# A fused graph-attention and mixture-of-experts kernel: VectorE's step without a cast, an addition and three signals; weights loaded by expert; two blocks' rows sent among the last dispatches

## The reference

```python
# layer 1, graph attention on the layer-normalised x
Wh = h @ W;  e = leaky_relu(Wh @ a[:D] + (Wh @ a[D:]).T, 0.2)
alpha = softmax(where(adj > 0, e, -inf));  x = x + elu(alpha @ Wh)
# layer 2, mixture of 8 experts on the layer-normalised x, the best 2 of each token
scores = h @ Wg.T + bg;  top2, idx = top_k(scores, 2);  p = softmax(top2)
x = x + sum over the two experts e of  p_e * (relu(h @ W1[e].T + b1[e]) @ W2[e].T + b2[e])
```

## Time and profile before

| | before |
|---|---|
| median of 3 runs | 440.71 us (440.66 to 441.59) |
| profiled execution | 442.13 us, span 440.3 us |
| busy: TensorE / VectorE / ScalarE / GpSimd | 407.3 / 358.9 / 321.3 / 289.0 us |
| mean granted TensorE clock | 0.991 |
| transfers | 63.04 MB |
| chain that ended last | TensorE 63%, VectorE 20%, ScalarE 5%, DMA 5%, issue 4% |

### The profile page before, as it was taken

One profiled execution on the slowest core, in us unless ns is written; L12 is line 12 of the kernel. 1 busy time (PEld: TensorE's weight loads), 2 busy tenths in 40 slices (PEclk: granted clock), 3 DMA queues, 4 the chain that ended last, 5 costly groups with the idle time before them and its releaser, 6 DMA issues.

```text
span 440.3 us, 9161 instructions
## 1 busy us (share of the span) xinstructions
PE 407.3 (93%) x2272; PEld 308.3 (70%) x2290; DVE 358.9 (82%) x1410; ACT 321.3 (73%) x760; POOL 289.0 (66%) x292
## 2 busy tenths in 40 slices
PE   7998999889998888999999999999999999999980
PEld 3656666666666665688878888888888888876630
DVE  5689999999998898999887887777778778757683
ACT  2678887888888987688888678778767877866500
POOL 1041777777777777777777777767667657764662
PEclk9999999999999999999999999999999999999996
DMA  5995334333333344443632433322233233297888
GB/s 181 293 390 193 102 115 118 108 103 104 100 101 104 97 128 122 128 133 98 200 99 95 122 102 101 115 90 84 91 90 90 66 84 90 79 289 247 248 310 316
DMA packets 44004, 63.04 MB, mean 143 GB/s; under 512 B 7744, under 2 KB 24512, under 8 KB 43712
## 3 DMA queue, kind: packets, MB, share of 16 engines
q1 hardware_dynamic: 30448, 34.88, 26.5%
q0 software_dynamic: 9344, 20.10, 13.6%
q10 hardware_dynamic: 4176, 7.66, 5.3%
HBM read 27.28 MB, written 26.94 MB: 123 GB/s over the span
## 4 chain that ended last, share of the span: by engine, by line
PE 63%; DVE 20%; ACT 5%; DMA 5%; issue 4%; SPq 1%; POOL 1%; DVEq 0%; ACTq 0%; POOLq 0%
PE bank L1441 7%; PE bank L1455 7%; PE bank L1454 7%; PE bank L1457 7%; PE bank L1445 7%; PE bank L1442 7%; PE bank L1425 3%; PE bank L1433 3%; PE bank L1403 3%; PE bank L1316 3%; DVE xn L1066 3%; PE bank L1401 3%; DVE bn L901 2%; DVE neg_max L1048 2%; DVE score L1043 2%
## 5 line engine op out<-in xcount | busy, mean ns | idle before, releaser
L520 POOL DMA_INDIRECT expert_slots<-rows,slot_i x128 | 126.4, 987 | 55.4 <-issue 33.5
L712 ACT ACTIVATE yb<-bank,b_sb 128x512 f32<-128x512 f32 x36 | 24.8, 688 | 51.8 <-PE bank L1457 51.8
L1454 PE MATMUL bank<-hh,w_hi 128*128 128x512 f32 x144 | 60.1, 417 | 0.0
L1441 PE MATMUL bank<-xh,w_hi 128*128 128x512 f32 x144 | 58.5, 406 | 0.9 <-ACT xh L697 0.5
L1455 PE MATMUL bank<-hh,w_lo 128*128 128x512 f32 x144 | 57.4, 398 | 0.0
L1445 PE MATMUL bank<-xl,w_hi 128*128 128x512 f32 x144 | 56.9, 395 | 0.2 <-DVE xl L1122 0.2
L1457 PE MATMUL bank<-hl,w_hi 128*128 128x512 f32 x144 | 56.8, 395 | 0.3 <-DVE hl L1153 0.3
L1442 PE MATMUL bank<-xh,w_lo 128*128 128x512 f32 x144 | 56.8, 395 | 0.0
L536 POOL DMA_INDIRECT moe_rows<-hrelu,ysi x40 | 41.2, 1030 | 17.6 <-issue 10.7
L536 POOL DMA_INDIRECT moe_rows<-hexp,ysi x40 | 40.9, 1023 | 17.7 <-issue 10.1
L1146 DVE CAST hh<-z 128x512 fp32r<-128x512 f32 x36 | 16.5, 459 | 42.3 <-ACT z L702 41.9
(11 more groups left out here) (166 smaller groups left out, 1051.0 us busy)
## 6 DMA issues: line engine op xcount, KB each, us to landing
rows<-xn SPq DMA_DIRECT2D x32, 256.0 KB
xs<-expert_slots SPq DMA_DIRECT2D x27, 260.0 KB
x_all<-x SPq DMA_DIRECT2D x16, 256.0 KB, 3.5
w_raw<-w_t SPq DMA_DIRECT2D x2, 2048.0 KB, 13.7
w_raw<-moe_rows SPq DMA_DIRECT2D x16, 256.0 KB, 4.5
out<-x_all ACTq DMA_DIRECT2D x16, 256.0 KB, 4.7
xs<-expert_slots ACTq DMA_DIRECT2D x11, 260.0 KB
w_hi<-moe_rows SPq DMA_DIRECT2D x9, 256.0 KB, 4.1
```

Of the source, the lines that this page charges most:

```text
L520: nc.gpsimd.indirect_dma_start(out=slots, out_offset=bass.IndirectOffsetOnAxis(ap=slot_i[q][:, k * SUB + j:k * SUB + j + 1], axis=0), in_= ...
L712: nc.scalar.activation(yb[:, :], ps_y[:, :], ACT.Identity, bias=b2_sb[:, e:e + 1]).then_inc(yb_ok, 1)
L1441: nc.tensor.matmul(ps_h[c][:, :], w1_hi[:, e, chunk], xh[:, :], start=True, stop=False)
L1454: nc.tensor.matmul(ps_y[:, :], w2_hi[:, e, c, :], hh[:, c, :], start=c == 0, stop=False)
```

## The change

Four edits. On VectorE, the chosen experts' numbers are compared as the 32-bit integers that the top-8 search delivers, without a copy to float32; the two variances of a step lie in one buffer and get their epsilon in one instruction in place of two; and the three signals to `met` are gone. On SyncE, the weights are loaded expert by expert, two transfers of 256 KB behind each of the first eight groups' row copies, in place of two of 2 MB ahead of them; the loop of copies is written out. On GpSimd, the rows of block 0 are sent after the dispatches of group 14, and the rows of block 1 between the two halves of group 15's dispatches, instead of after all dispatches; sends from block 2 on follow. ScalarE's wait for the weights counts eight transfers.

```diff
+            for g in range(SURE_GROUPS + 1):
+                pass_on(g // 2, g % 2)
+                if g < E:
+                    sp.dma_start(w1_raw[:, g, :], w1_t[:, g, :]).then_inc(c_w1, 16)
+                    sp.dma_start(w2_raw[:, g, :, :], w2_t[:, g, :, :]).then_inc(c_w2, 16)
...
+                    dispatch(gr, 0, q)
+                    if gr == GROUPS - 1:
+                        send_rows(1, 1)
+                    elif t <= GROUPS:
+                        pool.wait_ge(prob_t_ok, t)
+                    dispatch(gr, 1, q)
+                    if gr == GROUPS - 2:
+                        send_rows(0, 0)
...
+            for b in range(2, BUFS):
+                send_rows(b, b)
+            with pool.Fori(1, QUADS) as m:
...
-                dve.sem_inc(met, 1)
...
-                last = nc.vector.tensor_scalar(var2[:, 0, :], mv2[:, :, 1], EPS, None, ALU.add)
+                n = norms(gx)
+                nc.vector.tensor_scalar(var2[:, 0:n, :], mv2[:, 0:n, :, 1], EPS, None, ALU.add).then_inc(var2_ok, 1)
                 if norms(gx) > 1:
-                    last = nc.vector.tensor_scalar(var2[:, 1, :], mv3[:, :, 1], EPS, None, ALU.add)
-                last.then_inc(var2_ok, 1)
...
-                nc.vector.tensor_copy(top_f[:, :, :], top_i[:, :, 0:2].rearrange("p t k -> p k t")).then_inc(topf_ok, 1)
-                dve.wait_ge(topf_ok, gl + 1)
                 nc.vector.tensor_tensor(chosen[:, :, :, :], expert_no,
-                                        top_f[:, :, :, None].to_broadcast([P, 2, SUB, E]), ALU.is_equal
+                                        top_i[:, :, 0:2].rearrange("p t k -> p k t")[:, :, :, None].to_broadcast([P, 2, SUB, E]), ALU.is_equal
                                         ).then_inc(chosen_ok, 1)
...
-                nc.vector.tensor_tensor(above[:, :], top_f[:, 0, :], top_f[:, 1, :], ALU.is_gt).then_inc(above_ok, 1)
+                nc.vector.tensor_tensor(above[:, :], top_i[:, :, 0], top_i[:, :, 1], ALU.is_gt).then_inc(above_ok, 1)
```

More of the change, by code:

```diff
@@ L133, in gnn_moe_kernel @@
         bn3 = sb("bn3", [P, SUB, 6])
-        mv3 = sb("mv3", [P, SUB, 2])
         mean1 = sb("mean1", [P, GROUPS, SUB])
@@ L137, in gnn_moe_kernel @@
         bn2 = sb("bn2", [P, SUB, 6])
-        mv2 = sb("mv2", [P, SUB, 2])
+        mv2 = sb("mv2", [P, 2, SUB, 2])
         var2 = sb("var2", [P, 2, SUB])
@@ L165, in gnn_moe_kernel @@
         gap_1 = sb("gap_1", [P, SUB])
-        top_f = sb("top_f", [P, 2, SUB])
         above = sb("above", [P, SUB])
@@ L286, in gnn_moe_kernel @@
         gap1_ok = sem("gap1_ok")
-        topf_ok = sem("topf_ok")
         above_ok = sem("above_ok")
@@ L297, in gnn_moe_kernel @@
         rank_ok = sem("rank_ok")
-        met = sem("met")
         slotp_ok = sem("slotp_ok")
@@ L507, in _ @@
             pool.wait_ge(sure_out, 16 * SURE_BLOCKS)
[L509 to L525, removed]
             def send_rows(i, b, landings=()):
@@ L538, in send_rows, with dispatch, step @@
                         in_=ys[b][:, t, :], in_offset=None).then_inc(scattered[b], 16)
+            def dispatch(gr, k, q):
+                for j in range(SUB):
+                    nc.gpsimd.indirect_dma_start(
+                        out=slots, out_offset=bass.IndirectOffsetOnAxis(
+                            ap=slot_i[q][:, k * SUB + j:k * SUB + j + 1], axis=0),
+                        in_=rows[q][:, k, j, :], in_offset=None).then_inc(rows_out[q], 16)
+            def step(t, groups, q, m):
+                gr = groups[4]
+                if gr is not None:
+                    pool.wait_ge(slot_ok, gr + 1)
+                    pool.wait_ge(rowx_ok, 32 * (gr + 1))
+                    pool.sem_inc(stood, 1)
+                    dispatch(gr, 0, q)
[6 more added lines that the diff above has]
+                        send_rows(0, 0)
+            by_steps(pool, step)
             def pool_sum(g):
@@ L544, in pool_sum @@
                 nc.gpsimd.tensor_tensor(x2, x2, moe_in(0, g), ALU.add).then_inc(pool_sum_ok, 1)
-            with pool.Fori(0, QUADS) as m:
+            for b in range(2, BUFS):
+                send_rows(b, b)
+            with pool.Fori(1, QUADS) as m:
                 for b in range(BUFS):
@@ L574, in high_halves @@
             def high_halves(e):
-                act.wait_ge(c_w1, 16)
-                act.wait_ge(c_w2, 16)
+                act.wait_ge(c_w1, 16 * E)
+                act.wait_ge(c_w2, 16 * E)
                 nc.scalar.copy(w1_hi[:, bass.ds(e, 1), :].rearrange("p e h -> p (e h)"),
@@ L913, in second_var @@
                 dve.wait_ge(stats2_ok, gx + 1)
-                dve.sem_inc(met, 1)
                 for j in range(SUB):
-                    last = nc.vector.bn_aggr(mv2[:, j, :], bn2[:, j, :])
+                    last = nc.vector.bn_aggr(mv2[:, 0, j, :], bn2[:, j, :])
                 if norms(gx) > 1:
                     for j in range(SUB):
-                        last = nc.vector.bn_aggr(mv3[:, j, :], bn3[:, j, :])
+                        last = nc.vector.bn_aggr(mv2[:, 1, j, :], bn3[:, j, :])
                 last.then_inc(aggr2_ok, 1)
                 dve.wait_ge(aggr2_ok, gx + 1)
-                last = nc.vector.tensor_scalar(var2[:, 0, :], mv2[:, :, 1], EPS, None, ALU.add)
+                n = norms(gx)
+                nc.vector.tensor_scalar(var2[:, 0:n, :], mv2[:, 0:n, :, 1], EPS, None, ALU.add).then_inc(var2_ok, 1)
                 if norms(gx) > 1:
-                    last = nc.vector.tensor_scalar(var2[:, 1, :], mv3[:, :, 1], EPS, None, ALU.add)
-                last.then_inc(var2_ok, 1)
-                if norms(gx) > 1:
-                    nc.vector.tensor_copy(mean1[:, bass.ds(gx + AHEAD, 1), :].rearrange("p g s -> p (g s)"), mv3[:, :, 0]
+                    nc.vector.tensor_copy(mean1[:, bass.ds(gx + AHEAD, 1), :].rearrange("p g s -> p (g s)"), mv2[:, 1, :, 0]
                                           ).then_inc(mean1_ok, 1)
@@ L992, in second_shift @@
                 dve.wait_ge(rstd2_ok, gx + 1)
-                nc.vector.scalar_tensor_tensor(shift[:, :], mv2[:, :, 0], -1.0,
+                nc.vector.scalar_tensor_tensor(shift[:, :], mv2[:, 0, :, 0], -1.0,
                                                rstds[:, bass.ds(gx, 1), 0, :].rearrange("p g s -> p (g s)"), ALU.mult, ALU.mult
```

2 lines of the change are left out of this document (removed).

## The result

The median went from 440.71 to 446.01 us (5 runs each): ratio 1.0118, 95% interval 1.0085 to 1.0151: slower, by 1.2%.

The account below looks back on a forecast made before the run. Three loops of one length (VectorE's chain, TensorE's loop, a full GpSimd) were taken to bound phase 1. TensorE gains 3.4 us, but block 8 goes on 0.63 us later than before: 440.71 plus 0.6, 441.3 us, range 437.9 to 443.4.

Parts of the forecast that it names:

- VectorE's step: Steady steps of phase 1: VectorE saves 0.50 us a step, so TensorE reaches its blocks 3.4 us earlier.
- second loop: Phase 1: TensorE's scores, ScalarE's normalisation and exponentials, the product, the ranking; only 0.26 us shorter than VectorE's chain.
- Weights: Loads by expert on SyncE behind row copies: nothing on the path; GpSimd's fifth dispatch 0.5 us earlier, not 2.
- GpSimd's pace: Dispatches in phase 1: GpSimd is full, a dispatch lengthens 0 to 0.08 us, taken as 0; dispatching ends at 218.38.
- Sends and load: Before block 8: eight sends delay dispatching's end 10.22 us; load issued 6.56 us after it, landing 2.85 us later.
- The clock rival: At block 8, TensorE's clock falls in the 4.0 us idle stretch, costing 1.9 us: 443.2 us; chance 0.17.
- The offset stays: From block 8 to 414 us TensorE is busy throughout, so its 0.63 us lateness carries on: + 0.6 us.

Follow-up runs that it names:

- PSUM run: The changed kernel with one operand of VectorE's three fused instructions taken from a PSUM bank instead of SBUF: 440.70 us, ratio 1.0011.
- runs of dispatches by themselves: No kernel computation: sections of 16 GpSimd dispatches, each beside one repeated VectorE instruction, 512 then 448 columns; 0.96 us each with VectorE idle.

## Why the prediction was wrong

*VectorE's step, right.* 0.5 us a step and a second loop of 9.90; the rankings gained 3.4 us by 136.15, where 3.1 was forecast. At the last ranking 2.6 were left (185.57 against 188.15), for the wait of 2.62 us on dispatches. With the collisions gone, 3.6.

*Weights, right*: nothing (440.69 us alone, ratio 0.9993). GpSimd's fifth dispatch came 0.81 us earlier (46.26), 0.5 was taken.

*GpSimd's pace: the step that failed.* The prediction priced a lengthened dispatch at 0 to 0.08 us, looked for it in the weights' transfers, and took 0; its range allowed GpSimd's pace 1 us either way. It read 0.966 us from the earlier trace rows as the dispatch's own length, when it held only for one phase: with steps of 10.16 us and eight dispatches a dispatch began 0.61 us into `u` in each steady step, when `u` was all but done. With 0.26 us off the step one dispatch of each step began 0.1 to 0.2 us into `u` or `score` and took 1.3 to 1.45 us. From the fifth dispatch to the last's end, less the eight sends, GpSimd needed 175.08 - 10.2 = 164.9 us, before 161.6; of the 3.3 us between, the long dispatches make 2.9 (4.8 less 1.9). Dispatching ended at 221.34 instead of 218.38. The PSUM run and the runs of dispatches by themselves show that this is the cause: with the same step and the same sends, and one operand from PSUM, dispatching ended at 217.75.

*Sends and load: right to half a microsecond.* 6.08 us from the last dispatch to the load (6.56 taken), some 3.0 from load to rows (2.85). TensorE turned the rows at 230.48 instead of 227.79.

*The clock rival came true.* Idleness was 5.92 us instead of 4.0 (2.7 by the rows, less 0.8 by TensorE's later arrival). The price of 1.9 us was met in sum only: 1.25 are the clock's. In the PSUM run it fell behind 3.55 us, less than the forecast's own 4.0, so 0.17 was too low a chance. The rule cited from the Trainium skill (TensorE: Matmul & The Clock Gate, Part 1) agrees with the falls at 3.55, 3.83 and 5.92 us of idleness.

*The offset stays: off by 1.7 us.* Between the profiled executions it shrank from 4.91 at block 9 to 3.20 at the last block: the blocks behind took 6.43 us against 6.46, and before had one of 7.77 us. The PSUM run shows what luck there is in a sum like this one: TensorE stood 1.2 us behind before at block 9 (235.15 against 233.92), where the forecast without the clock's fall has 0.6, and 0.35 us ahead at the last block. Its 440.70 us beside the forecast's 441.3 come of two errors that cancel, the clock and the offset.

## What to carry to other kernels

When two engines run loops of equal length, their phase is part of the tuning: a duration read from such a trace is that of one phase, and shortening one loop asks what the other's instructions will now meet. Before a queue that is full is delayed by 10 us, its end is to be priced with its worst dispatch, and a dense stage's idle stretch with the clock behind it. Where a long VectorE instruction with two SBUF operands meets GpSimd's dispatches and a PSUM bank can be freed, one operand from PSUM is worth a try: it took this change from 446.01 to 440.70 us.

## What the runs showed of the hardware

A dispatch of 128 rows by GpSimd takes 0.96 us and a pause of 0.30. It takes up to 1.51 us when it begins under a VectorE instruction of 512 columns that reads two SBUF operands, by the time that is left of the instruction; a reduction of one SBUF operand did not lengthen it. Beside unbroken instructions a dispatch with its pause stretches to a whole number of them: with three of 448 columns the dispatch takes 1.30, with four copies 1.01 or 1.08. One operand from PSUM frees it (0.96 us), with the instruction hardly shorter (0.608 us against 0.611).

The Trainium skill (SBUF — State Buffer, Who interferes with whom) says that VectorE and GpSimd share a port pair: a VectorE instruction with two SBUF inputs contends for it with a GpSimd instruction that reads SBUF, one in a two-port mode, as copies can be, with GpSimd altogether, and whichever comes second blocks until the first is done. The sections with 1.30 us and those with copies agree. It also reports that an addition of two tensors did not stall GpSimd's transfers; for these indirect ones the 1.34 and 1.30 us differ, and the measurement decides.

TensorE's granted clock stayed at 1.00 over an idle stretch of 2.17 us and fell to 0.50 (1.2 GHz) within one of 5.92 us and just behind ones of 3.55 and 3.83.
